# Clearing a finished stage's semaphores inside the next stage's block

## What is computed

```python
x = x + axial_attention(_gn(x), ...)        # L0: two linear attentions, along rows and columns
x = x + attention_rel_pos(_gn(x), ...)      # L1: 16 heads, softmax, relative positions
t = tokens(x)
t = t + attention_ln(_ln_t(t), ...)         # L2: softmax attention, residual, layer norm
t = t + experts_top1(_ln_t(t), ...)         # L2: 8 experts, one per token
t = t + attention(_ln_t(t), ...)            # L3
t = t + experts_top4(_ln_t(t), ...)         # L3: shared expert and 4 of 8 routed ones
```

## Time and profile before

| what | us |
|---|---|
| median of 3 runs | 2035.12 |
| lowest and highest | 2034.88, 2040.15 |
| span of the profiled execution | 2036.8 |
| TensorE, VectorE, ScalarE, GpSimd busy in it | 1562.8, 1269.2, 779.2, 785.0 |

### The profile page before, as it was taken

The page is one execution under the profiler, slowest core; times in us unless marked ns, Lnnn a source line. Parts: engine busy times, 40 slices in busy tenths (PEclk is TensorE's granted clock), DMA queues, the critical chain, the costliest instruction groups (busy, mean ns, idle before and its releaser), DMA issues. The chain is left out here.

```text
span 2036.8 us, 38838 instructions
## 1 busy us (share of the span) xinstructions
PE 1562.8 (77%) x13148; PEld 1212.7 (60%) x13148; DVE 1269.2 (62%) x2435; ACT 779.2 (38%) x1652; POOL 785.0 (39%) x956
## 2 busy tenths in 40 slices
PE   5958577649997587791285879947996999999990
PEld 3536464527774344461053546526886999999990
DVE  4846456566664665558224688675664777777776
ACT  2311012305453133451021336622114777777770
POOL 1531102360001440002222250014885887878770
PEclk8968788859998778895598879977997999999995
DMA  2465543354311633219331443114115656666545
GB/s 91 164 166 161 146 115 102 115 168 121 99 48 63 189 84 74 64 19 317 113 88 62 125 141 96 42 39 131 61 65 183 241 206 240 210 229 226 213 156 206
DMA packets 286766, 274.02 MB, mean 135 GB/s; under 512 B 59034, under 2 KB 263677, under 8 KB 280959
## 3 DMA queue, kind: packets, MB, share of 16 engines
q1 hardware_dynamic: 260535, 229.35, 36.3%
q10 hardware_dynamic: 17376, 21.31, 3.3%
q0 software_dynamic: 8688, 21.16, 2.8%
HBM read 194.74 MB, written 79.35 MB: 135 GB/s over the span
## 5 line engine op out<-in xcount | busy, mean ns | idle before, releaser
L787 DVE TENSOR_REDUCE a_maxima<-psum 128x2 f32<-128x512 f32 x384 | 257.5, 687 | 156.4 <-PE psum L578 88.7
L758 ACT ACTIVATE a_probs<-psum 128x512 f32<-128x512 f32 x384 | 224.6, 598 | 262.0 <-PE psum L600 167.8
L89 PE MATMUL psum<-e_x_split,e_up_split 128*128 128x256 f32 x2340 | 311.5, 282 | 7.4 <-DVE e_x_split L1749 7.4
L89 PEld LDWEIGHTS psum<-e_x_split,e_up_split 128*128 128x128 f32 x2340 | 292.5, 189 | 7.8 <-DVE e_x_split L1749 7.8
L1793 POOL TENSOR_TENSOR e_up_split<-e_up_raw,e_up_split 128x512 fp32r<-128x512 f32 x195 | 252.6, 1296 | 90.2 <-ACT e_up_split L1715 88.4
L1685 PE MATMUL psum<-e_down_split,e_hidden_split 128*128 128x256 f32 x1170 | 173.5, 284 | 0.4 <-DVE e_hidden_split L1775 0.4
L578 PE MATMUL psum<-s_k_stack,s_q_stack 96*128 96x256 bf16 x512 | 123.0, 295 | 41.6 <-DMA a_rel_stack<-scr_r 29.7
L1685 PEld LDWEIGHTS psum<-e_down_split,e_hidden_split 128*128 128x128 f32 x1170 | 152.5, 188 | 0.6 <-DVE e_hidden_split L1775 0.6
L1770 DVE TENSOR_TENSOR psum<-psum,e_silu 128x256 f32<-128x256 f32 x195 | 83.8, 430 | 106.8 <-ACT e_silu L1736 106.7
L1754 DVE TENSOR_TENSOR e_down_split<-e_down_raw,e_down_split 128x256 fp32r<-128x256 f32 x195 | 146.3, 750 | 0.0
L1039 DVE TENSOR_TENSOR a_products<-psum,mask 128x512 f32<-128x512 f32 x128 | 82.9, 686 | 78.6 <-PE psum L972 78.4
(11 more groups left out here) (247 smaller groups left out, 3178.1 us busy)
## 6 DMA issues: line engine op xcount, KB each, us to landing
e_up_raw<-in_w_ffn SPq DMA_DIRECT2D x39, 1280.0 KB, 7.4
e_down_raw<-in_w_ffn SPq DMA_DIRECT2D x39, 640.0 KB, 4.2
scr_q<-p_parts SPq DMA_DIRECT2D x40, 384.0 KB, 2.7
scr_k<-p_parts SPq DMA_DIRECT2D x40, 384.0 KB, 2.8
a_q_stack<-scr_q SPq DMA_DIRECT2D x96, 128.0 KB, 2.9
s_q_stack<-scr_q SPq DMA_DIRECT2D x96, 128.0 KB, 2.7
s_k_stack<-scr_k SPq DMA_DIRECT2D x96, 128.0 KB, 2.7
a_k_stack<-scr_k SPq DMA_DIRECT2D x84, 128.0 KB, 3.0
```

The source lines that it names most:

```text
L89: last = eng.matmul(out, lhs(a, k), rhs(b, k), start=i == 0, stop=i == len(terms) - 1)
L758: act.activation(PB[:, u % PR], st_bank(u), ACT.Exp, scale=0.25).then_inc(S["probs"], 1)
L787: dve.tensor_reduce(MX[:, u // 8, :, u % 8], s_bank(u), AX.X, ALU.max).then_inc(S["s_used"], 1)
```

## The change

The block in `Phase.__exit__` is gone. A phase that ends is noted in a list with its semaphores, and `clear_finished(sp)`, which each kind of stage now calls at one place of SyncE's code, clears whatever is in the list. The names of the semaphores are given back only when the phase that cleared them has ended as well. Behind the whole program one block is left that clears what is still listed.

```diff
     def __exit__(self, *e):
-        if e[0] is None:
-
-            with self.nc.Block() as block:
-                @block.sync
-                def _(sp):
-                    for s in self.sems:
-                        sp.sem_clear(s)
+
         self.ctx.close()
+        for names, _ in Phase.cleared:
+            names.close()
+        Phase.cleared = []
+        Phase.over.append((self.names, self.sems))
+
+
+def clear_finished(sp):
+
+    for _, sems in Phase.over:
+        for s in sems:
+            sp.sem_clear(s)
+    Phase.cleared += Phase.over
+    Phase.over = []
...
                     for dst, src in loads:
                         sp.dma_start(dst, src).then_inc(w_loaded, 16)
+                clear_finished(sp)
                 if loads:
                     sp.wait_ge(w_loaded, 16 * len(loads))
...
+                    if n == 0:
+                        clear_finished(sp)
                 if scr_v is not None:
...
                     step(0, first=True)
+                    clear_finished(sp)
                     with sp.Fori(1, IMAGES - 2) as i:
...
                         load_stack(sp, b, j)
+                clear_finished(sp)
...
                         sp.dma_start(T[rows, axis, :, rows], table).then_inc(placed[axis], 16)
+                clear_finished(sp)
                 for c in range(HALVES):
...
                     sp.dma_start(BG[:], bias.partition_broadcast(P)).then_inc(loaded, 16)
+                clear_finished(sp)
                 if scr_g is not None:
...
                     sp.dma_start(gates_of(m)[j * rest:end], row).then_inc(S["gates_loaded"], 16)
+                clear_finished(sp)
                 sp.wait_ge(scattered, 16 * TOP * TILES)
...
                 load_weights(1)
                 load_x(2)
+                clear_finished(sp)
                 for i in range(2, packs):
...
+                clear_finished(sp)
                 for done in scattered:
                     sp.wait_ge(done, 16)
...
+    with nc.Block() as block:
+        @block.sync
+        def _(sp):
+            clear_finished(sp)
+
...
                     sp.dma_start(GB[:, i, :], v.partition_broadcast(P)).then_inc(loaded, 16)
+                clear_finished(sp)
```

More of the change, by code:

```diff
@@ L45 @@
 class Phase:
+    over, cleared = [], []
     def __init__(self, nc, name):
-        self.nc, self.name, self.ctx, self.sems = nc, name, ExitStack(), []
+        self.nc, self.name, self.ctx, self.names, self.sems = nc, name, ExitStack(), ExitStack(), []
     def sem(self, name):
-        s = self.ctx.enter_context(self.nc.semaphore(f"{self.name}_{name}"))
+        s = self.names.enter_context(self.nc.semaphore(f"{self.name}_{name}"))
         self.sems.append(s)
@@ L2011, in program @@
     scr["v"] = nc.dram_tensor("scr_v", [TOKENS, D], F32, kind="Internal").ap()
+    Phase.over, Phase.cleared = [], []
     with ExitStack() as ctx:
```

## The result

| | before | after | ratio |
|---|---|---|---|
| first comparison, 4 runs each | 2035.43 | 2005.91 | 0.9849, interval 0.9828 to 0.9871 |
| second, 17 and 5 runs | 2037.28 | 2013.22 | 0.9881, interval 0.9862 to 0.9900 |
| third, 10 and 5 runs | 2036.6 | 2011.1 | 0.9873, interval 0.9846 to 0.9900 |

The account below looks back on a forecast made before the run. No engine is always busy; all five wait between the 23 chained stages. Gain 27.4 - 0.8 (a3) - 0.1 (a5) - 0.5 (pauses) = 26.0 us, so 2035.12 - 26.0 = 2009.1 us; range 2005.5 to 2013.

Parts of the forecast that it names:

- The seams: Between stages: 27 blocks removed give 5.7 us, 344 clears moved 19.3, five pauses in SyncE's clears 2.4; together 27.4 us.
- Pauses that come back: In SyncE's stream: pauses removed at stage ends may fall elsewhere, costing 0 to 2.4 us; 0.5 us taken.
- Normalise, project, route, shared, streamed: In these stages clears stand where SyncE only waits or is idle, or nothing is held up: cost nothing.
- a3 and a5: Clears between attend's first image and the loop make SyncE late: 0.8 us lost in a3, 0.1 us in a5.
- Stages keep their length: In every stage but a3: its own length, first instruction to last, changes by no more than 1 us.
- rival 1: TensorE's loop in attend: moved code makes a back edge dear or cheap, 3.2 us either way, 2012.3 or 2005.9; chance 0.08.
- rival 2: Attend's small loops: 12 taken VectorE back edges turn dear at 3.2 us each, 38.4 us, time 2047.5; chance 0.02.
- Rival 3: SyncE becomes the bound in more places than a3 and all pauses return: gain 21.1 us, time 2014.0; chance 0.05.
- Rival 5: Next block's end waits for SyncE's clears: gain 5.7 us, 2029.4; chance 0.04, with anything leaving less than half.
- Rival 4: Something older, such as transfers issued in f3 for e4, holds a stage's start: 3.1 us not gained, 2012.2; chance 0.03.

Follow-up runs that it names:

- the experiment with 48 clears: The changed kernel with one clear for each run of neighbouring semaphore numbers, not one for each semaphore: ratio 0.9857.
- clears first: The changed kernel with the clears as the first thing in SyncE's part of every stage, ahead of its loads: ratio 0.9890.
- the two with attend's at the end: The changed kernel with attend's clears behind SyncE's last step, once with each issued ten times (0.9867), once with one clear per run of neighbouring semaphore numbers (0.9850).
- ten times the clears: The changed kernel with each clear between attend's first image and the loop issued ten times: ratio 0.9991.

## Why the forecast was near and the range was not

**The seams: right, in the sum and in the split.** 27.4 us forecast, 28.0 measured. The prices hold: in the kernel before, 0.21 us a block and 0.056 a clear give 0.88 us for a seam with 12 clears, 0.99 for 14 and 1.88 for 26 in two blocks, and the seams without a pause measure 0.88 (n0), 1.00 (p3) and 1.88 (a3). Neighbouring clears start 53 to 56 ns apart, pauses aside, before and after. Only blocks with few clears are dearer than the formula, 0.32 us with one, since there the barrier waits for TensorE's drain and not for SyncE's. About half of the missing 0.6 us is a sixth pause, which the rows of line 69 could not show: behind n6 the 12 clears take 0.6 us as usual, but GpSimd, which gathers the signals and gives the release, takes 0.38 us between the two where it takes 0.08 behind n0, and the seam is 1.19 us and not 0.88.

**Pauses that come back: not shown.** I put 0.5 us. In the changed kernel's first profile two pauses stand among the clears inside stages, of 0.4 us each, in n3 (621 us) and n6 (1303 us), and nobody is seen to wait for them. Late starts do stand among SyncE's transfers (below). What they cost there no run tells. Nor does any run show that a pause is the crossing of a fetch block, as the prediction took it to be beside its first rival.

**Normalise, project, route, shared, streamed: right.** Their clears cost nothing by the experiment with 48 clears: with 302 clears fewer inside the stages none of these stages is more than 0.4 us shorter than in the changed kernel's profiles. That the place is what makes it free shows in f3, 3.4 us longer with the clears ahead of two loads.

**a3 and a5: right mechanism, wrong rows, size not shown.** I put a3's cost at 0.8 us and read it from the wait of 6.52 us at 781.99. That is the third image's wait: the loop begins at about 747 us, and the back edge behind its first turn (772.7) I took for its start. The wait behind the place of the clears, in the kernel before and in the changed one:

```profile
756.02 0.39 PE L600 MATMUL psum<-a_q_stack,a_k_stack 98*128 98x256 bf16 x2 [0.68 <-DMA a_q_stack<-a_max_rows]
```

```profile
738.22 0.39 PE L612 MATMUL psum<-a_q_stack,a_k_stack 98*128 98x256 bf16 x2 [1.50 <-DMA a_q_stack<-a_max_rows]
```

The waits differ by 0.8 us, but that is no proof of the forecast's 0.8: counted from the stage's start both matmuls begin at the same time, 53.39 and 53.35 us. The transfer came no later; TensorE was only done sooner with what stood ahead of it. The better comparison is with the three kernels that have no clears there (clears first, and the two with attend's at the end). They issue this pair of transfers 47.9 to 48.3 us from the stage's start, the changed kernel 49.20 and 49.08 (first and third profile). So the clears do put the transfer off, by 0.8 to 1.3 us. What the stage loses by it is not told: a3 is 213.7, 215.4 and 215.7 us without clears there and 215.8 and 215.9 with them. Of the two with attend's clears at its end, the one with a wait of 1.22 us has the shorter a3, 215.4 us, and the one without a wait 215.7.

In the second profile of the changed kernel the same wait is this:

```profile
741.84 0.61 PE L612 MATMUL psum<-a_q_stack,a_k_stack 98*128 98x256 bf16 x2 [5.79 <-DMA a_q_stack<-a_max_rows]
```

That is 4.3 us more in one program, and most of why its a3 was 6 us longer. The long a3 is not the change's doing: the kernel before with each semaphore cleared twice, which has no clear inside a stage, has it too, 219.7 us with a wait of 4.50 us at this place. In a5 the single clears cost nothing that can be told from the spread: the wait at the place where ten times the clears made 7.57 us is 0.81 us before, 0.20 in each profile of the changed kernel and 0.18 with the clears at the stage's end.

**Stages keep their length: this step failed.** I wrote that none but a3 would change by more than 1 us, and the sum puts every other stage at nothing. p3 and p5 became 1.7 us shorter each, since TensorE's clock was at its high level in their first 4 us where it had been low behind a seam, and the block put back behind n3 and n5 makes both long again (59.9 and 51.6 us). I had priced a seam by its length alone. h6 became 1.0 to 1.8 us longer, and VectorE's cast of the hidden rows is where it shows, in the kernel before (line 1501) and in the changed one (line 1517), with the same 32 casts:

```profile
L1501 DVE CAST h_hidden_split<-h_hidden 128x512 fp32r<-128x512 f32 x32 | 37.7, 1178 | 6.2 <-PE psum L1424 3.4
```

```profile
L1517 DVE CAST h_hidden_split<-h_hidden 128x512 fp32r<-128x512 f32 x32 | 41.6, 1301 | 6.2 <-PE psum L1440 3.5
```

It goes with the missing block ahead of h6 and not with the clears inside the stage. With the clears inside but the blocks kept, h6 is 149.4 us (one clear in the block) and 148.4 us (12), and the casts take as long as before:

```profile
L1523 DVE CAST h_hidden_split<-h_hidden 128x512 fp32r<-128x512 f32 x32 | 37.6, 1175 | 6.4 <-PE psum L1446 3.7
```

Why the casts take longer without the seam stays open.

**The sum: near, in part by luck.** 26.0 us forecast, 26.9 by the mean ratio, 26.2 by the means of all runs (2010.7 and 2036.9). But the seams and the three stages that changed in every profile make 28.0 + 3.4 - 1.5 = 29.9 us. So the terms that I left out come to some 4 us more, and some 3 us were lost again in stages that differ from one execution to the next. Whether any of these 3 us is a cost of the change no run tells.

**The range: the step that put the time outside it.** The spread of one program's executions was put at nothing, and the stages' own gain of 1.9 us (3.4 - 1.5) was too. The range of 7.5 us was made of uncertain terms alone, with the four runs that the first ratio rests on taken as exact. Their own spread was 8.7 us (2003.0 to 2011.7), and the interval of their ratio 8.8 us wide. The kernel before had shown 5.3 us between three runs and I let it stand. The first ratio asks for 2004.4 us, 1.1 us below the range, and its interval reaches from 2000 to 2009: so the miss itself is within the noise of four runs. With a spread of 5 us on either side, taken together with the range's own 3.75 as independent errors (6.2 us), the range would have been 2003 to 2015, and held it.

**The rivals.** The loops' back edges hardly changed: the dear one stayed where it was, in a3, at 3369 ns before and 3669, 3519 and 3554 after, though all the code had moved. So it does not go with the place in the code, and rival 1 is out; VectorE's 15 branches take 50 to 74 ns, so rival 2 is too. TensorE's row, to be held against the earlier trace rows:

```profile
L715 PEldq COMPARE_BRANCH  x6: 76/155/3669, 524.5 to 1279.1; - x6
```

The Trainium skill, "Runtime: NRT & Kernel Launch", section "Instruction fetch mechanics", has a taken branch wait for a fetch when its target is outside the part of the program held on the engine; the page gives TensorE's store 2,048 instructions. In the changed kernel's trace a turn of the loop has 1,414 instructions in a2, 2,185 in a3 and 1,030 in a5, matmuls and weight loads counted singly, and only a3's is dear, in agreement with the page. That length and not something else in a3 makes it so was not tried. Rival 3 holds for a3 as to who issues late, not as to its size. Rival 5 is excluded by the 0.33 us at the seams. Rival 4 would have given back in e4 the 3.1 us that the seams ahead of it lost. e4 is 120.3, 122.1 and 122.2 us after and 120.2 and 120.1 before, and the 2 us of the long ones go with TensorE's clock (see below).

## What to carry to other kernels

- Work that all engines wait for costs its time in full, each time and exactly; the same work in one engine's queue costs nothing or, ahead of a transfer that someone waits for, more than itself (7.4 us of clears made 10 to 12 us of a5). So ask of a moved step what is behind it in the queue, and test the answer with ten times as much of it.
- An idle seam ahead of a stage of matmuls can also cost by TensorE's clock behind it: here 1.7 us for 0.9 us of seam at p3 in five profiles of five, at p5 in three of five.
- A range needs the executions' own spread beside that of the terms. Here the exact part of the profile repeats to 0.01 us, while the stages sum to 1998 to 2009 us in one program. Ask for the before kernel's spread over many runs, not three.
- A wait that grew is no proof that what it waits for came later. Compare when it ended, counted from the stage's start.

## What the runs showed of the hardware

- One program has two lengths in some stages: e4 120.3 and 122.2 us, a2 196 and 198.4, a3 216 and 221.9. In e4 and a2 TensorE's busy time goes along (72.9 and 75.0; 183.5 and 186.3), with a mean clock of 0.80 and 0.78, 0.96 and 0.94. In a3 it is mostly the wait shown above. The long a3 also came in the kernel before with every clear doubled. What makes an execution take the one or the other stayed open.
- SyncE's transfers, too, start late now and then, by 0.6 and 1.1 us here, and not at the same transfer each time: among the loads of a3's second and third image, which start 0.65 us apart, one start was followed by the next after 1.24 us in the changed kernel's first profile (24.40 to 25.64 us from the stage's start), and the one before it by the next after 1.77 us in its second (23.75 to 25.52), the one with the long a3.
- A block in which SyncE alone has one clear costs all five engines 0.32 us, one with 12 clears 0.88. Neighbouring clears start 53 to 56 ns apart, twice the 25 ns that each one's row gives.
- Five of the 348 distances between neighbouring clears in the kernel before are 0.38 to 0.49 us. Behind n6 such a pause stands in GpSimd's stream between the last signal and the release, 0.38 us.
